# State-space projections: the steps' projection ahead, softplus by a corrected logarithm, two piece tiles, broadcast rows on 3 partitions

## What is computed

```python
x = x + _L0_attn_ref(_L0_cond_ref(x, cond_1024, ...), ...)   # _L0_cond_ref: tanh recurrent network
# _L0_attn_ref(x): BATCH 16, seq 128, DIM 128, d_inner 256, d_state 128, one head
xz = jnp.einsum('btd,ed->bte', x, in_proj_w)
x_inner, z = jnp.split(xz, 2, axis=-1)
x_conv = _silu(causal_conv4(x_inner, conv_w) + conv_b)
x_dbl = jnp.einsum('btd,ed->bte', x_conv, x_proj_w)
dt, Bm, Cm = x_dbl[..., :1], x_dbl[..., 1:129], x_dbl[..., 129:]
dt = jax.nn.softplus(jnp.einsum('bth,dh->btd', dt, dt_proj_w) + dt_proj_b)
A_mean = jnp.mean(-jnp.exp(A_log), axis=0)
# scan over t:
h = jnp.exp(dt_t[:, :, None] * A_mean) * h + dt_t[:, :, None] * B_t[:, None, :] * u_t[:, :, None]
y_t = jnp.einsum('bds,bs->bd', h, C_t)
# afterwards:
y = y * lax.rsqrt(jnp.mean(jnp.square(y), axis=-1, keepdims=True) + eps) * norm_w
return jnp.einsum('btd,od->bto', y * _silu(z), out_proj_w)
```

## Time and profile before

| | |
|---|---|
| median of 3 runs | 7361.7 us (7357.31 to 7364.68) |
| the profiled execution | 7363.88 us |
| its span | 7362.1 us |
| its mean granted TensorE clock | 0.942 |
| TensorE busy | 5760.5 us, 78% of the span |
| VectorE busy | 5820.5 us, 79% |
| ScalarE busy | 4421.0 us, 60% |
| GpSimd busy | 2712.0 us, 37% |

### The profile page before, as it was taken

How to read it: one execution, slowest core, us unless ns; L and a number is a source line. 1 busy time by engine, 2 the same in 40 slices (tenths; PEclk the granted TensorE clock), 3 DMA queues, 4 the chain that set the end, 5 groups by cost and what they waited for, 6 DMA issues and landing times. The chain is left out here.

```text
span 7362.1 us, 151269 instructions
## 1 busy us (share of the span) xinstructions
PE 5760.5 (78%) x49639; PEld 3129.6 (43%) x49913; DVE 5820.5 (79%) x11267; ACT 4421.0 (60%) x9397; POOL 2712.0 (37%) x2033
## 2 busy tenths in 40 slices
PE   5877787787778777877787707888888887943989
PEld 3555454455445555544454402333333333531543
DVE  4888988898889888988898669999999995455333
ACT  6877877787778777877787604444444442323322
POOL 2222222222222222222222108999999992000000
PEclk9999999999999999999999859999999998976989
DMA  0000000000000000000000010000000000000000
GB/s 7 2 2 2 2 2 2 2 2 2 2 2 2 2 2 2 2 2 2 2 2 2 10 34 5 4 4 4 4 4 4 4 4 3 0 10 3 0 17 6
DMA packets 14180, 30.30 MB, mean 4 GB/s; under 512 B 3665, under 2 KB 11602, under 8 KB 12434
## 3 DMA queue, kind: packets, MB, share of 16 engines
q1 hardware_dynamic: 13586, 22.47, 1.1%
HBM read 15.12 MB, written 7.34 MB: 3 GB/s over the span
## 5 line engine op out<-in xcount | busy, mean ns | idle before, releaser
L421 ACT ACTIVATE rx_junk<-rx_z 128x384 bf16<-128x384 f32 x2178 | 1371.9, 638 | 0.3
L1005 POOL TENSOR_TENSOR hc<-hh,cg 128x512 f32<-128x512 f32 x1024 | 1277.0, 1267 | 80.4 <-DVE hh L987 75.0
L927 ACT ACTIVATE ps_m<-ps_m,aneg 128x508 f32<-128x508 f32 x1024 | 673.6, 658 | 946.0 <-DVE hh L987 828.7
L987 DVE TENSOR_TENSOR_SCAN hh<-ps_m,bx 128x512 f32<-128x512 f32 x1024 | 1214.0, 1209 | 13.8 <-POOL bx L1009 13.8
L506 POOL TENSOR_TENSOR rx_z<-rx_z 128x512 f32<-128x512 f32 x256 | 384.9, 1504 | 2204.6 <-ACT rh_z L437 2201.5
L891 PE MATMUL ps_m<-hc,pick 128*128 128x512 f32 x2048 | 1056.3, 599 | 9.8 <-POOL hc L1005 8.5
L641 DVE TENSOR_REDUCE rh_ends<-rh_z 128x4 f32<-128x1536 f32 x512 | 960.3, 1919 | 131.0 <-ACT rh_z L437 131.0
L337 PE MATMUL r_ps<-rx_z,negid 128*128 128x256 f32 x2192 | 565.7, 405 | 280.2 <-POOL xsl L549 189.3
L512 POOL TENSOR_TENSOR rx_z<-rx_z 128x1024 f32<-128x1024 f32 x274 | 656.5, 2396 | 73.4 <-DVE rx_z L607 36.7
L313 PE MATMUL r_ps<-rh_z,negid 128*128 128x256 f32 x2048 | 496.8, 384 | 166.2 <-ACT r_ps L432 163.6
L337 PEld LDWEIGHTS r_ps<-rx_z,negid 128*128 128x128 f32 x2192 | 422.8, 202 | 391.0 <-issue 326.6
(11 more groups left out here) (397 smaller groups left out, 10726.0 us busy)
## 6 DMA issues: line engine op xcount, KB each, us to landing
rows_scratch<-pc SPq DMA_DIRECT2D x48, 128.0 KB
rows<-rows_scratch SPq DMA_DIRECT2D x128, 48.0 KB
ew<-in_e SPq DMA_DIRECT2D x3, 1024.0 KB, 7.0
rh_z<-in_x_dn SPq DMA_DIRECT2D x1, 1024.0 KB, 4.8
xcur<-in_x_dn SPq DMA_DIRECT2D x1, 1024.0 KB
out_x<-xcur SPq DMA_DIRECT2D x1, 1024.0 KB, 3.9
qi<-in_f_q SPq DMA_DIRECT2D x1, 384.0 KB, 2.9
xpw<-in_xp_t SPq DMA_DIRECT2D x1, 257.0 KB
```

The lines of the kernel that those rows point to most:

```text
L421: e.activation(junk[:, n % JUNK], xz[i][:, :, n, 2:K2].rearrange("p c k -> p k c"), ACT.Copy, accum_out=xsum[:, i, n:n + 1]).then_inc(x_fo ...
L927: e.activation(da[un % NDA][:, :, 1:T], ps[:, un % 2, :].rearrange("p (n t) -> p n t", n=NG4)[:, :, 1:T], ACT.Exp, scale=aneg[:, 0:1]).the ...
L987: e.tensor_tensor_scan(hh[un % NBUF][:], da[un % NDA].rearrange("p n t -> p (n t)"), bx[un % NBUF][:], 0.0, ALU.mult, ALU.add).then_inc(sc ...
L1005: e.tensor_tensor(hc[un % NHC][:], hh[un % NBUF][:], cg[:], ALU.mult).then_inc(weighted, 1)
```

## The change

In the preparation:

- The first three loads have a semaphore of their own and are what the input projection waits for; the other six count on `loaded2`, and the residual is waited for only ahead of the last additions of the third block.
- There are two tiles, one per half, for the convolution's input (`xi0`, `xi1`), its output, the logarithm, its inverse and the pieces (`pc0`, `pc1`). Scratch for the halves lies in `yh`, which the scan fills later. The input projection's groups alternate between two sets of four banks.
- TensorE issues the step's projection (L740) and its spreading (L745) ahead of B's and C's projections (L751).
- Softplus: ScalarE makes |z|, e = exp(-|z|), max(z, 0), ln(u) of u = 1 + e, and exp(-ln(u)) in place of a reciprocal; VectorE corrects: ln(u) - ((u - 1) - e) * exp(-ln(u)).
- The turn from t, n to n, t is done in the addition that makes dt and in the product that makes w; casts (on ScalarE) and subtractions (on VectorE) then run along the columns.
- SP stores each piece in 4 DMAs as soon as it is cast, and waits once, at the end, for all 48.
- B's copies (ScalarE) come between the casts of the halves, C's copies go to VectorE, at its end.

In the scan: the row tiles and `ones3` have 3 partitions instead of 128, and the zero-fills are gone.

```diff
-                     e.wait_ge(loaded, 160)
+                    e.wait_ge(loaded, 48)
+                    for h in range(4):
                         for c in range(4):
+                            if h >= 2:
+                                e.wait_ge(a, A_AT[f"xi{h - 2}{c}"])
+                            e.matmul(ps[:, 4 * (h % 2) + c, :], win[:, h * 128:(h + 1) * 128], hs[:, col(c)],
                                      start=True, stop=True).then_inc(m, 1)
...
+                    def absolute(h):
+                        e.wait_ge(m, M_AT["dt"] + 4 * h + 4)
+                        after("uu1")
+                        z = ps[:, 4 * (1 - h):8 - 4 * h, :].rearrange("p a b -> p (a b)")
+                        did(f"abs{h}", e.activation(ee[h], z, ACT.Abs, bias=dtb[:, h:h + 1]))
+                        after(f"abs{h}")
+                        did(f"exp{h}", e.activation(ee[h], ee[h], ACT.Exp, scale=-1.0))
+                    def positive(h):
+                        did(f"relu{h}", e.activation(relu[h], z, ACT.Relu, bias=dtb[:, h:h + 1]))
+                    def logarithm(h):
+                        did(f"ln{h}", e.activation(ln[h][:], up[h], ACT.Ln))
+                        did(f"inv{h}", e.activation(inv[h][:], ln[h][:], ACT.Exp, scale=-1.0))
...
+                        did(f"u{h}", e.tensor_scalar(up[h], ee[h], 1.0, None, ALU.add))
+                        did(f"n{h}", e.scalar_tensor_tensor(out=up[h], in0=up[h], scalar=-1.0, in1=ee[h],
+                                                            op0=ALU.add, op1=ALU.subtract))
+                    def product(h):
+                        did(f"p{h}", e.tensor_tensor(up[h], up[h], inv[h][:], ALU.mult))
+                    def log1p(h):
+                        did(f"r{h}", e.tensor_tensor(ln[h][:], ln[h][:], up[h], ALU.subtract))
+                    def step(h):
+                        did(f"dt{h}", e.tensor_tensor(rows_of(steps[h]), by_n(relu[h]), by_n(ln[h][:]), ALU.add))
+                    def drive(h):
+                        did(f"w{h}", e.tensor_tensor(rows_of(drives[h]), rows_of(steps[h]), by_n(uu[:, h, :]), ALU.mult))
...
-            rows = [[ss(f"rows{q}{b}", [128, CH, W4], BF16) for b in range(2)] for q in range(2)]
-            ones3 = ss("ones3", [128, 128], BF16)
+            rows = [[ss(f"rows{q}{b}", [3, CH, W4], BF16) for b in range(2)] for q in range(2)]
+            ones3 = ss("ones3", [3, 128], BF16)
...
-                                e.dma_start(rows[q][b][0:3].rearrange("p a b -> p (a b)"),
+                                e.dma_start(rows[q][b][:].rearrange("p a b -> p (a b)"),
...
-                    e.memset(ones3[:], 0.0).then_inc(grp, 1)
+                    e.memset(ones3[:], 1.0).then_inc(grp, 1)
...
-                    for q in range(2):
-                        for b in range(2):
-                            e.memset(rows[q][b][:], 0.0).then_inc(grp, 1)
-                    e.wait_ge(grp, NDA + 8)
-                    e.memset(ones3[0:3, :], 1.0).then_inc(grp, 1)
+                    e.wait_ge(grp, NDA + 4)
...
+                    e.wait_ge(residual, 16)
```

More of the change, by code:

```diff
@@ L752, in _ @@
+                    for h in range(H2):
                         for c in range(4):
                             e.wait_ge(m, 8 + 4 * h + c + 1)
[L754 to L762, removed]
@@ new lines, in _ @@
+                    absolute(0)
+                    positive(0)
+                    absolute(1)
+                    logarithm(0)
+                    positive(1)
+                    did("aneg", e.activation(aneg[:], alog[:], ACT.Exp))
+                    logarithm(1)
+                    for h in range(H2):
+                        for part in ("hi", "mid", "lo"):
+                            for q in "dw":
+                                cast(part, q, h)
+                        if h == 0:
+                            for c in range(4):
+                                e.wait_ge(m, M_AT["bc"] + c + 1)
+                                did(f"bm{c}", e.activation(bm[:, :, c * 32:(c + 1) * 32].rearrange("p n t -> p t n"),
+                                                           ps[:, 4 + c, :].rearrange("p (t n) -> p t n", n=N), ACT.Copy))
@@ new lines, in remove @@
+                    def remove(k, q, h):
+                        part = ("hi", "mid")[k - 1]
+                        e.wait_ge(a, A_AT[f"{part}{q}{h}"])
+                        after(f"w{h}")
+                        if k == 2:
+                            after(f"d1{q}{h}")
+                        src = whole[q][h] if k == 1 else left[q][h]
+                        did(f"d{k}{q}{h}", e.tensor_tensor(left[q][h], src, pc[h][:, Q[q], k - 1, :], ALU.subtract))
+                    product(0); log1p(0); step(0); drive(0)
@@ new lines, in _ @@
+                    remove(1, "d", 0)
+                    product(1)
+                    remove(1, "w", 0)
+                    log1p(1)
+                    remove(2, "d", 0)
+                    step(1)
+                    remove(2, "w", 0)
+                    drive(1)
+                    for k in (1, 2):
+                        for q in "dw":
+                            remove(k, q, 1)
+                    e.wait_ge(a, A_AT["aneg"])
+                    did("aneg", e.tensor_scalar(aneg[:], aneg[:], -1.0, None, ALU.mult))
```

239 lines of the change are left out of this document (117 added, 122 removed).

## The result

The changed kernel takes 8564.1 us (median of 4 runs, 8557.9 to 8569.8), against 7359.9 us before in runs beside it: a ratio of 1.1635, 95% interval 1.1615 to 1.1655. It is slower by a sixth. The profiled execution took 8557.9 us, its span is 8556.1.

What follows compares the result with a forecast made beforehand. GpSimd and VectorE pace the scan, TensorE's spare room rests on the clock, and the preparation is a serial chain. 7363.9 - 132 (preparation) + 1388 (scan) = 8620 us; likeliest case 8470 to 8790, full range 7300 to 8790.

Steps and rivals of the forecast that it cites:

- its likeliest case: Scan at the half clock nearly throughout: 8620 us, range 8470 to 8790, chance 74%.
- What bounds the scan: GpSimd and VectorE set the pace; TensorE's 1.29 us a unit hides behind 1.57 at the full clock only.
- The preparation: State-space module ahead of the scan: first L907 at 4309 against 4441.8, about 132 us saved (115 to 145).
- the strided addition: VectorE's dt in the new layout, in the preparation: 3.66 us by L832, or 2.29 if strides cost nothing.
- The switch: Scan, one way in and out between 3-row and 128-row matmuls per unit: 0.43 us half clock, 0.30 full.
- 8-row pairs of the last module: L1618, f32, between 128-row pairs: 2.00 us at the half clock, the following pairs 1.86 and 1.71.
- The clock: Scan stays at the half clock, 2.99 us a unit, until a pass's last six state sums; scan grows 1388 us.
- The step from one-row matmuls to three-row broadcasts: L735's one-row work, busy 6.99 of 7.0 us, stayed at clock 0.50; the same taken for 3 rows.
- each restart loses the clock again: At a pass's start broadcasts run alone; the first state sum took 1.91 us, the half-clock duration, even before the change.
- The row taken for such a mixture: Last module, pairs around 8-row L1618: no gap, yet the last still took 1.71 us; later pairs 1.02 to 1.12.
- The clock stays up: Rival: busy TensorE suffices whatever the rows; scan unit 1.59 us, time 7252 us (7232 to 7345); 18%.
- A clock that returns in part of each pass: Rival: L891 restores the clock in some passes or partway, units average 1.59 to 2.99 us; 7400 to 8400 us; 6%.

Runs made afterwards that it cites:

- burst: Changed kernel plus 24 matmuls over 128 rows, into an unused bank, once a pass ahead of its first state sum: 7305.9 us.
- 64 rows: Changed kernel with row tiles and `ones3` on 64 partitions, zero-filled, instead of 3: 7294.6 us.
- half of the edit: Changed kernel with 128-partition tiles, dt's broadcast over 128 rows and w's over 3: 7266.6 us.

## Why the prediction was right

The forecast was 8620 us, slower, with 8470 to 8790 for its likeliest case, and 8564 was measured. By its steps:

*What bounds the scan.* Right. The spare room of TensorE rested on the clock; with the clock gone TensorE is busy without a gap and the other engines wait, as the windows show.

*The preparation: 132 us forecast, 137.6 in the profile.* The order of events was the forecast one. Counted from the first load issue, TensorE began at 4.5 us (5.5 forecast), the first absolute value stood at 42.1 (44.5), ScalarE's stretch took 25.7 us (26.4), the second half's first cast ended at 102.9 (107.5), and the first broadcast came at 131.7 (136.5). No single term is off by more than 1.5 us, and nearly all are off in the same sense; why was not tried. The price that had been in doubt, the strided addition, is 3.65 us (3.66 taken from L832).

*The switch.* 0.43 us at the half clock was forecast from the 8-row pairs of the last module, 2.97 - 2.56 = 0.41 measured; 0.30 at the full clock was forecast and measured (burst, 64 rows). That the numbers agree so closely is partly luck: they were picked inside 0.29 to 0.59 and 0.15 to 0.39, from f32 pairs, and with one broadcast over 3 rows in place of two the same way in and out costs 0.22 and 0.21. The Trainium skill, page "TensorEngine Tiling (Array Packing)", Key Properties, has a change of tiling mode drain TensorE; that a matmul over 3 rows is such a change no run here shows, but the traces agree that going there and back costs something: 0.21 to 0.30 us at the full clock, 0.22 to 0.41 at the half.

*The clock.* Right in its result: half speed for all but the ends of the passes. The step from one-row matmuls to three-row broadcasts held, and so did the step that each restart loses the clock again. The step was a bet, though: the earlier trace rows show seven us of one-row work alone, and no row of before has 3 rows between wide pairs. The row taken for such a mixture does not bear it out, for the stretch ends at 7137.5 and the granted clock is 1.00 from 7138 on. And half of the edit shows that one narrow broadcast a unit does not keep the clock down. One thing in the reasoning was left too wide: the prediction took from L735 that narrow work "did not raise the clock" and did not part raising the clock from holding it. The burst shows a mixture that holds the clock once it has it. That made no difference to the time, because every pass here began its state sums at the half clock.

The Trainium skill, page "TensorE: Matmul & The Clock Gate", Part 1 (What's actually happening), ties the clock to how busy TensorE has been; in the changed scan it is busy without a gap for 191 us of 191 behind the first state sum at a clock of 0.50, so that busy time alone does not decide here.

*The sum.* A pass was put at 382 us and took 377 (period of the blank pairs, (6939.3 - 4676.9) / 6 = 377.1): 2.8 us of it from 2.967 us a unit in place of 2.99, 2.4 from the last state sums, which regain the clock sooner, less 0.5 for a longer restart. Over the scan, 8 x 382 = 3056 against 3014.9, that is 41 of the 62 us between the forecast and the profiled run; the preparation has nearly 6, the scan of before, at 1674 and not 8 x 208.5 = 1668, another 6, and the program's other stages the 9.5 named above.

*The rivals.* The clock stays up (18%) describes what the 64-row version does, with the unit of 1.59 us that it named: there the scan warms up in each pass, as before the change. At 3 rows it did not happen. A clock that returns in part of each pass (6%) came in no version in the form that was priced, with a quarter of the units slow or more.

## What to carry to other kernels

Zeros that make a matmul full height are not wasted where the granted clock is at stake: 17 us of zero-fills kept a 1674 us scan from becoming 3015. Before a contraction is narrowed, read from the trace what the clock does while narrow matmuls run alone (a sign and no proof: with half of the edit the clock came back), and what each engine's time per unit would be at the half clock; here TensorE had room at 1.29 us and none at 2.56. And of an edit that comes along with a larger one, cost it on its own: the preparation's rewriting was worth 1.6% and stood, and the row edit cost eleven times that.

## What the runs showed of the hardware that was not expected

- The clock has a memory in a loop: one sequence of matmuls (two broadcasts over 3 rows, one f32 pair over 128) ran at 0.50 for 191 us on end in one kernel and at 1.00 for 173 us in the other, where 24 matmuls over 128 rows stood ahead of it. A short stretch of work can so decide the time of a long one: 192 matmuls in all were worth 1258 us.
- The number of rows that a matmul contracts over acts on the clock at equal durations: 3 and 64 rows take the same 0.60 to 0.63 us at the half clock and 2.97 us a unit, yet with 64 the clock came back in each pass, 3 to 20 us after its first state sum, and with one of two broadcasts at 128 after 3 to 11; with 3 it came back in none before the broadcasts ended.
- A change of form costs 0.21 us there and back at the full clock when a bf16 matmul over 128 rows follows, and 0.30 when the way out leads into a pair with f32 weights; 64 rows cost this as 3 do (1.59 us a unit).
